# Four interleaved streams in place of three, with extra products in the differential attention's steps

## The reference

```
x += attn0(norm(x))   # causal, 8 heads of 16, with a bias of head directions ("geo")
x += ffn0(norm(x))    # 8 experts, top 1, hidden 512                          ("moe0")
x += attn1(norm(x))   # differential: per token, 32 x 32 scores over heads of 4,
                      # two softmaxes, one minus lambda times the other, rmsnorm ("diff")
x += relu mlp(norm)   # hidden 512 (part of the same layer)                    ("ff")
x += ffn1(norm(x))    # rows and weights quantised to a 6-bit grid in blocks of 32 ("mx")
x += attn2(norm(x))   # 16 heads of 8, q, k, v, o with low-rank additions      ("lora")
x += ffn2(norm(x))    # 14 experts, top 1, hidden 256                         ("moe2")
x += attn3(norm(x))   # causal, 16 heads, 128-wide q and k, values of 8        ("wide")
out = x + ffn3(norm(x))  # 8 experts, top 1 with a capacity over all tokens, hidden 128 ("moe3")
```

## Time and profile before

| | us |
|---|---|
| median of three runs | 3001.14 |
| profiled execution, its own time | 2994.16 |
| its span, first to last instruction | 2992.9 |
| PE / DVE / ACT / POOL busy | 1949.1 / 1711.6 / 1148.7 / 667.2 |
| granted TensorE clock, mean | 0.757 |
| one of the six three-stream rounds | 323.3 to 328.4 |

### The profile page before, as it was taken

One profiled execution on the slowest core, in us unless ns is written; L12 is line 12 of the kernel. 1 busy time (PEld: TensorE's weight loads), 2 busy tenths in 40 slices (PEclk: granted clock), 3 DMA queues, 4 the chain that ended last, 5 costly groups with the idle time before them and its releaser, 6 DMA issues. The chain is left out here.

```text
span 2992.9 us, 42119 instructions
## 1 busy us (share of the span) xinstructions
PE 1949.1 (65%) x12945; PEld 1395.1 (47%) x12945; DVE 1711.6 (57%) x4319; ACT 1148.7 (38%) x2756; POOL 667.2 (22%) x900
## 2 busy tenths in 40 slices
PE   4540655588756785598657876679559866666483
PEld 3330442456454564466444655456346635443352
DVE  2337545666584667665675668466766667552132
ACT  0320323255433463265333553355325543243251
POOL 1015002500243103500251014310350025201101
PEclk9875865688757895699668985699569876785795
DMA  6120040304141322305140324223230514011402
GB/s 177 37 78 0 13 122 6 111 6 102 52 120 40 64 73 77 100 7 125 33 138 13 73 70 115 57 42 96 69 108 1 126 34 133 15 23 44 128 1 60
DMA packets 265524, 201.28 MB, mean 67 GB/s; under 512 B 29668, under 2 KB 238692, under 8 KB 264708
## 3 DMA queue, kind: packets, MB, share of 16 engines
q1 hardware_dynamic: 259124, 185.59, 24.1%
q0 software_dynamic: 6144, 12.60, 1.5%
HBM read 151.58 MB, written 35.52 MB: 63 GB/s over the span
## 5 line engine op out<-in xcount | busy, mean ns | idle before, releaser
L1607 DVE TENSOR_REDUCE mid_room<-ps 128x2 f32<-128x512 f32 x256 | 165.2, 688 | 104.1 <-PE ps L944 101.2
L1200 ACT ACTIVATE late_room<-ps 128x384 f32<-128x384 f32 x256 | 125.9, 492 | 244.2 <-PE ps L875 242.3
L1212 ACT ACTIVATE late_room<-ps,late_neg_max 128x128 f32<-128x128 f32 (+1 forms) x512 | 187.3, 421 | 32.1 <-DVE late_neg_max L1582 27.6
L1047 PE MATMUL ps<-mid_pool 128*128 128x128 f32 x544 | 134.0, 390 | 97.4 <-DMA mid_pool<-moe_small 60.1
L1246 ACT ACTIVATE mid_room<-ps 128x512 f32<-128x512 f32 x256 | 140.2, 595 | 94.8 <-PE ps L955 94.8
L1763 DVE TENSOR_TENSOR early_pool<-ps,early_pool 128x1024 f32<-128x1024 f32 x128 | 150.8, 1220 | 37.2 <-ACT early_pool L1302 32.7
L1047 PEld LDWEIGHTS ps<-mid_pool 128*128 128x128 f32 x544 | 107.6, 275 | 122.1 <-DMA mid_pool<-moe_small 73.9
L865 PE MATMUL ps<-late_aT,heads_T 128*128 128x256 f32 x512 | 162.2, 400 | 0.0
L1284 ACT ACTIVATE mid_room<-ps,mid_pool 128x128 f32<-128x128 f32 x272 | 85.2, 364 | 188.8 <-PE ps L1047 188.1
L1770 DVE TENSOR_REDUCE early_pool<-early_pool 128x256 f32<-128x1024 f32 x128 | 149.8, 1212 | 1.3
L1581 DVE TENSOR_REDUCE late_neg_max<-ps 128x1 f32<-128x128 f32 x256 | 73.6, 287 | 125.8 <-PE ps L867 124.7
(11 more groups left out here) (374 smaller groups left out, 5088.0 us busy)
## 6 DMA issues: line engine op xcount, KB each, us to landing
mid_pool<-in_m_w_dram SPq DMA_DIRECT2D x272, 128.0 KB, 2.1
early_pool<-m_folded_w SPq DMA_DIRECT2D x88, 256.0 KB, 3.3
early_pool<-in_m_w_dram SPq DMA_DIRECT2D x88, 256.0 KB, 3.2
mid_pool<-mid_room SPq DMA_DIRECT2D x192, 64.0 KB
heads_T<-in_m_w_dram SPq DMA_DIRECT2D x176, 64.0 KB, 1.9
mid_pool<-moe_small SPq DMA_DIRECT2D x136, 65.0 KB, 1.9
mid_room<-moe_sorted_in SPq DMA_DIRECT2D x32, 256.0 KB, 3.1
moe_sorted_out<-mid_room SPq DMA_DIRECT2D x32, 256.0 KB, 2.5
```

Of the source, the lines that this page charges most:

```text
L1047: mm = pe.matmul(ps[:, B + b % h_banks, c * P:(c + 1) * P], table[:, c * P:(c + 1) * P], rows_T[s][:, b, :], start=True, stop=True)
L1200: act.activation(probs_T[s][:, k % (2 * QUAD), :], ps[:, s.last_bank, 0:3 * P], ACT.Copy)\
L1212: ins = act.activation(probs[s][:, n % RING, qt, 0:w], ps[:, bank, qt * P:qt * P + w], ACT.Exp, bias=neg_max[s][:, n % RING, qt:qt + 1])
L1607: dve.tensor_reduce(all_max[:, :, (h % 2 * 8 + h // 2) * GROUP_SEQS + seq], ps[:, B + n % S_BANKS, :].rearrange("p (q k) -> p q k", q=2), ...
```

## The change

- A fourth stream, SECOND, with PSUM bank 2 alone, takes diff from EARLY and ff and mx from MID. EARLY keeps geo and moe0 with banks 0 and 1; MID keeps lora and moe2; LATE is as before. Each order string is new, and there is one more round: EARLY; EARLY, SECOND; EARLY, SECOND, MID; five rounds of all four; SECOND, MID, LATE; MID, LATE; LATE.
- The ring of score banks is `s.banks - 1` for the causal attentions: one bank for geo, two for wide. Lora keeps two. `h_banks` of moe0 becomes one.
- Diff's q, k and v are copied from the one bank to a ring of three in SBUF by ACT, and the next product may start when that is done. DVE reads q, k and v there, and multiplies and sums one quarter at a time, the sum waiting for the product. ff too uses one bank where it had two.
- In the ten steps of each of diff's five passes PE does two products of 128 x 512 in bfloat16 in most steps, into SECOND's bank between its uses, which nobody reads: 2 in each of four steps of all five passes, and 2 in each of two more steps of the last four, 56 in a round.
- Geo's q and k are copied whole, and PE takes the 17 rows of a head from them; the strips and POOL's clearing are gone. Values are packed without padding.
- A block's table is one DMA from a table laid out whole in DRAM in the preparation, into a ring of three. The tables of moe2 and moe3 are laid out by DMAs on ACT's queue beside the first round, and SP waits for them after it.
- In the causal attentions ACT copies the summed values after the exponentials of the step and not before.
- At a round's end there are three copies of x and none of z.

```diff
-TABLES = 4
-TABLE_DMAS = 3
+TABLES = 3
...
+    def score_banks(self, at):
+        return self.banks if at is LORA else self.banks - 1
...
-EARLY = Stream("early", 0, 3, ["geo_in", "geo_out", "moe0_router", "diff_in", "diff_out"],
-               ["v", "o", "conn"])
-MID = Stream("mid", 3, 2, ["diff_ff", "mx_in", "lora_in", "lora_out", "moe2_in"], ["ff", "mx", "v", "o"])
+EARLY = Stream("early", 0, 2, ["geo_in", "geo_out", "moe0_router"], ["v", "o"])
+SECOND = Stream("second", 2, 1, ["diff_in", "diff_out", "diff_ff", "mx_in"], ["conn", "ff", "mx"])
+MID = Stream("mid", 3, 2, ["lora_in", "lora_out", "moe2_in"], ["v", "o"])
 LATE = Stream("late", 5, 3, ["wide_in", "wide_out", "moe3_router"], ["v", "o"])
...
+    "ESML": (
+        "MLMMESELMLSEMMELSLEEMLSELEMSLLESLEMLLEMLMESLLMESMLMELMLELMELMLEMLMLEEMLEMLLMEMLMEMMMMMESMESMMSSME"
...
-                    sp.dma_start(tables[s][:, i, 0:m.w2_at], layer1[m][:, bass.ds(expert, 1), :]).then_inc(here, 16)
-                    sp.dma_start(tables[s][:, i, m.w2_at:m.b2_at],
-                                 layer2[m][:, bass.ds(expert * m.chunks, m.chunks), :]).then_inc(here, 16)
-                    sp.dma_start(tables[s][:, i, m.b2_at:m.width],
-                                 small[m][bass.ds(expert * P, P), :]).then_inc(here, 16)
+                    sp.dma_start(tables[s][:, i, :].unsqueeze(1), whole[m][:, bass.ds(expert, 1), :]).then_inc(here, 16)
...
+                    ring = s.score_banks(at)
+                    if k >= ring:
+                        before_kind, before_n = slots[k - ring]
...
+                    def keep_busy(n):
+
+                        for _ in range(n):
+                            pe.matmul(ps[:, B, :], ones_bf[:, :],
+                                      tri[:, :].unsqueeze(1).broadcast_to([P, BANK // P, P]), start=True, stop=True)
 
                     def qkv(t):
-                        if t >= 2:
-                            pe.wait_ge(qkv_used, t - 1)
-                        pe.matmul(ps[:, B + t % 2, 0:3 * DIM], aT[s][:, t * P:(t + 1) * P], diff_w[:, :],
+                        if t >= 1:
+                            pe.wait_ge(qkv_kept, t)
+                        pe.matmul(ps[:, B, 0:3 * DIM], aT[s][:, t * P:(t + 1) * P], diff_w[:, :],
                                   start=True, stop=True).then_inc(qkv_ready, 1)
...
+                        for _ in range(2):
+                            if t >= 1:
+                                keep_busy(2)
+                            yield
+                        if t + 1 < TILES:
+                            qkv(t + 1)
+                        yield from steps(4)
+                        pe.wait_ge(qkv_kept, min(t + 2, TILES))
+                        for _ in range(len(DIFF_PARTS) - 6):
+                            keep_busy(2)
+                            yield
...
                         settle()
-                        for i in quarters:
-                            tick(dve.tensor_tensor(
-                                prod[:, i % 2, :, :].rearrange("p (i j) d -> p i j d", i=n),
-                                q[:, i * n:(i + 1) * n, :].unsqueeze(2).broadcast_to(shape),
-                                k.broadcast_to(shape), ALU.mult))
...
+                        link(dve.tensor_tensor(
+                            prod.rearrange("p (i j d) -> p i j d", i=n, j=DIFF_Q),
+                            q[:, i * n:(i + 1) * n, :].unsqueeze(2).broadcast_to(shape),
+                            k.unsqueeze(1).broadcast_to(shape), ALU.mult))
+                        tick(dve.tensor_reduce(dscores[:, i * 256:(i + 1) * 256],
+                                               prod.rearrange("p (n d) -> p n d", d=DIFF_D), AX.X, ALU.add))
...
-        with nc.Fori(0, GROUPS - 2) as g:
+        with nc.Fori(0, GROUPS - 3) as g:
             with nc.Block(no_gpsimd_drain=True) as block:
-                group_block(block, [EARLY, MID, LATE], x_v[:, bass.ds(g * TILES + 2 * TILES, TILES), :],
+                group_block(block, list(STREAMS), x_v[:, bass.ds(g * TILES + 3 * TILES, TILES), :],
```

More of the change, by code:

```diff
@@ L285, in sequence_model @@
             rstd[s] = own("rstd", [P, 2, TILES])
-            v_pad[s] = own("v_pad", [P, TILES, heads, STRIP])
+        for s, at, m in ((EARLY, GEO, MOE0), (MID, LORA, MOE2), (LATE, WIDE, MOE3)):
+            own = lambda name, shape, dt=F32: sb(f"{s.name}_{name}", shape, dt)
+            v_pad[s] = own("v_pad", [P, TILES, at.heads * (at.v_depth + 1) + STRIP])
             inv_sum[s] = own("inv_sum", [P, 16, 1])
@@ L634, in _ @@
             def _(act):
-                act.wait_ge(lam_ready, 1)
+                act.wait_ge(prepared, LAM)
                 act.activation(lam_exp[:, :], lam_sum[:, :], ACT.Exp).then_inc(lam_exped, 1)
+                act.wait_ge(weights_here, LOADED)
+                for dst, src in later_copies:
+                    with nc.allow_non_contiguous_dma(reason="columns of tables, once"):
+                        act.dma_start(dst, src).then_inc(later_tables, 16)
             @block.vector
@@ L759, in early, with second @@
                     yield from experts(EARLY, MOE0)
-                    yield from steps(len(WEIGHTS[EARLY]) - len(causal_weights(EARLY, GEO))
-                                     - len(experts_weights(MOE0)))
+                def second():
+                    yield from steps(len(WEIGHTS[SECOND]))
                 def mid():
-                    yield from steps(len(FF_STEPS))
                     yield from steps(4)
@@ L804, in _ @@
                     sp.wait_ge(x_here, 16)
-                take_steps(streams, [early() if s is EARLY else mid() if s is MID else late() for s in streams])
+                programs = {EARLY: early, SECOND: second, MID: mid, LATE: late}
+                take_steps(streams, [programs[s]() for s in streams])
             @block.tensor
@@ L1105, in early @@
                     yield
-                def mid():
-                    s, B = MID, MID.bank
                     yield from steps(2)
```

359 lines of the change are left out of this document (180 added, 179 removed).

## The result

The changed kernel takes 2949.47 us (median of 4 runs, 2940.5 to 2953.44), the kernel before beside it 2998.9 (2990.37 to 3003.38). The ratio is 0.9865, 95% interval 0.9815 to 0.9914: faster by 1.35%, where 6.4% was forecast. It lies outside the forecast's own range (2720 to 2910) and nearest to the 2974 of the rival "little gained". The page of the changed kernel answers to the earlier trace rows.

A forecast was written before the change was run, and what follows sets the result against it. Too few independent chains for two in-order engines were taken as the bound. Rounds outside the full ones, 1346 us, plus five full rounds, 1455, made 2801; with span and run offsets 2809 us, 6.4% less, range 2720 to 2910.

The forecast's parts named there:

- little gained: Rival for the full rounds: rate only 1.42, 324 us a round, 2974 us in all; chance 0.15.
- The more independent chains stand in the string, the less often: Bound of the kernel before: in-order engines wait at their heads; rate 0.8, 1.1, 1.36 with one, two, three streams.
- With four I take 1.56: Five full rounds: PE plus DVE work over length 1.56, within 1.46 and 1.75, giving 291 us a round.
- up to 21 us: Geo's single score bank: up to 21 us more in EARLY alone, or in a full round if uncovered.
- under 8 us in a full round if hidden: Check on PE's waits for ACT's exponentials at the score products: under 8 us if hidden, over 20 for the slower rival.
- Slower: the single banks hold PE: Rival for the full rounds: rate stays 1.36, 345 us a round, 3079 us in all; chance 0.15.
- more than 40 us from 1346: Sign of a wrong prediction: rounds of filling summing to more than 40 us away from 1346.
- EARLY alone was 151: First round: 55 + 71 us for geo and moe0, plus up to 21 and 4 for single banks, 151.
- MID, LATE was 228: Round of MID and LATE without ff and mx: 144.8 + 83.6 = 228 us.
- Nothing in the sum: One DMA per table: 3 us gain a round (0 to 8), a ring of three giving some back (0 to 5).
- The work of DVE: Full rounds: DVE's quarters stay at 1.22 us each for product and sum; waiting adds up to 0.1 us x 16.
- The extra products: The 56 unread products in a full round: 18 us of PE as cost, 10 as gain by a better clock.

The follow-up runs named there:

- e6: Changed kernel with the ESML string of the full rounds replaced by one spreading each stream's steps evenly; 3233.33 us, 1.0784.
- e7: Kernel before, three streams, with its EML string replaced by an evenly spread one; 3448.78 us, 1.1512.
- e8: Kernel before with one score bank for geo, one for moe0's first layer, and ACT's copy of out_T behind the exponentials; 3157.45 us, 1.051.
- e9: Changed kernel with ACT's exponentials ahead of the copy of probs_T in geo; 2950.13 us, 0.9856.
- e4: Changed kernel with three banks for EARLY (two for scores) in the three rounds where LATE does not run; 2917.89 us, 0.9749.
- e15: e12 plus e14's ring of four and a third bank for MID in rounds where EARLY or LATE does not run; 2836.32 us, 0.946.
- e12: Changed kernel with the edits of e3, e4 and e5 together; 2875.96 us, 0.9611.
- e14: Changed kernel with a ring of four tables for moe2 and moe3, three kept for moe0; 2949.97 us, 0.9845.
- e13: Kernel before, ring of four tables kept, with each table fetched by one DMA from whole tables in DRAM; 2980.54 us, 0.9944.
- e3: Changed kernel with ACT's copy turning diff's v so that DVE reads it in order; 2934.53 us, 0.9816.
- e1: Changed kernel without the 448 products that nobody reads; 2941.46 us, 0.9839.
- e2: Kernel before with the same 56 unread products a round added in EARLY's last bank during diff; 2996.37 us, 1.0016.
- e5: Changed kernel with four steps of EARLY and SECOND moved ahead of six of MID's in ESML; 2946.23 us, 0.9824.
- e11: Changed kernel with each table fetched by three DMAs of column ranges, ring of three kept; 3054.32 us, 1.0205.

## Why the prediction was right in sign and wrong in size

**The mechanism.** "The more independent chains stand in the string, the less often" an engine stands still: PE plus DVE over length rose from 1.36 to 1.46, and with even orders the same step takes 34 us from a round (e6, e7). That much fits. That the fourth chain alone does it is not shown, since no run has four streams and nothing else changed. The sum over rounds is right as a method: of the seven parts outside, three came within 6 us.

**The step that failed** is "With four I take 1.56". The full rounds measured 1.46, 307.7 us instead of 291, which is 83 of the 149 us. The work in the sum was right (450 us for 454), so the error is the rate. It continued a series of 0.8, 1.1, 1.36 with "each added less than the one before", but the steps it names (0.26, then 0.26 to 0.3) do not get smaller, and the series says nothing of a fourth step that also takes banks away. Its own lower bound, 1.46, is what came.

Why the rate stopped there is open. The prediction had worked out a price of single banks, "up to 21 us" for geo and 13 for moe0, and put it "inside the 1.56", in no term of its own. In e8 single banks cost some 20 us in each round of three streams, and it shows as PE's wait for ACT at geo's score products (13.4 us). But e8 runs the order of the kernel before, which has two banks, and it moves ACT's copy of the summed values too, which no run tries alone. In the changed kernel's full round PE never waits for ACT at geo's score products; its waits for geo's exponentials come at the value products, 3.9 us in all, and moe0's first layer has no wait for ACT:

```profile
PE ps L897 <- ACT early_room L1233: 3.9, 3, 1.3
```

The check "under 8 us in a full round if hidden" therefore says hidden, and e9, which shortens the chain, wins nothing there. 307.7 less 20 would be 288, next to the 291 forecast, but that is arithmetic with a number of another order and not a finding. It may be that the new string bends around the single bank at a price that no row of waits shows; nothing here tests it. What the rows do show of PE's idle time in that round are waits for other things: 11.4 us for MID's normalised rows, 8.4 for SECOND's rows behind the quantised layer, 7.9 for tables, 7.6 for the rows of maxima.

**The rivals.** "Little gained" came nearest in time, 2974 us, with 1.42 and 324 us for a full round. It had too low a rate in the full rounds and too little time outside them, and the two partly cancel. "Slower: the single banks hold PE" had 345 us a round; its sign, over 20 us of waits for ACT at the score products, did not come.

**The rounds of filling.** By the prediction's own sign (more than 40 us from 1346) it is wrong here: 1412. EARLY alone was 151 and took 183.8. The chain of 2.6 to 2.7 us a unit is right to the tenth at the full clock. The terms carried over from the earlier trace rows are not: geo's stretch ran at 0.96 there and at 0.61 here, and took 97 us for 55, where 21 more were taken:

```profile
82.30:179.30 97.00, 62.00 (x248) 35.04 (x248) 17.71 (x62) 21.93 (x56) 1.28 (x2) 0.61 0.01 3
```

The prediction took PE's work as unchanged, and in e4, with two banks and PE never idle, the clock is at 0.50 all the same. Against the 126 us of the earlier trace rows the round is 58 longer, and e4 takes 31 of them back. Moe0 took some 85 us for 71, where 4 more were taken; PE waits 12.0 us for its tables in this round, 6.4 in the kernel before. MID, LATE was 228 and took 243.4: the forecast added up the lengths of lora's and moe2's stretches, in which PE is busy 138 us, while all of LATE's work falls into the new round, which has 164. EARLY, SECOND, MID was 260 and took 277.7, with 364 us of work at 1.31. That MID's two banks bind in both is what e15 says beside e12 (256.0 for 269.9 and 224.2 for 243.4), in which only the ring differs besides, and e14's ring alone left them at 276.9 and 239.5.

**Tables by one DMA.** "Nothing in the sum", with 0 to 8 us a round as bounds: measured 15.5 us in a full round, 17 in MID, LATE, 105 in the launch. The bound was made from PE's wait for tables with three streams (6.4 us), and there the saving is 2 us a round (e13), as taken. It was not asked what the transfers cost when a fourth stream's work stands in the same queues. PE's wait for tables did not fall to the 3 us expected; it is 7.9. Put together, the result comes apart as follows: four streams with three DMAs cost 59 us (3054.32 against 2995.64 beside it), and the one DMA gives 105 back. Without this term, which the sum had at nothing, the change would have been slower than the kernel before.

**The work of DVE** was taken as 1.22 us for each quarter. The product with v takes 2.07 from SBUF, and DVE is busy 217 us in a full round instead of 211. e3 takes that back without a gain that is clear of the noise.

**The extra products** were taken as 18 us of cost and 10 of gain. As PE time the net is right: PE is busy 7 us a full round more than in e1 (233.5 for 226.3), and the line of the 56 products in a full round reads:

```profile
L1098 PE MATMUL ps<-tri,ones_bf 128*128 128x512 bf16 x56 | 19.6, 458 | 0.0
```

On the clock the changed kernel has 0.85 in a full round and e1 0.83: it was high without them, probably because diff no longer stands alone. By the Trainium skill, "TensorE: Matmul & The Clock Gate", section "What's actually happening", activity is what releases the throttle. The trace of e2 agrees (0.77 to 0.84); the 32 us of e4 with PE always busy and the clock at 0.50 do not, and there the measurement decides. Neither says that the released clock buys time, and here it does not.

**Order.** The prediction left it out. The existing strings are worth 76 and 58 us a round against one even order each, in the launch far more than the whole change. Whether 1.56 could be reached by a better string is open: e5, one hand-made repair, won nothing that is clear of the noise.

## What to carry to other kernels

When a change adds a chain by taking buffers from the others, price the buffers as their own term and give it a sign; do not let it vanish in a rate read where the buffers were still there. Taking a buffer away alone prices it, but for the order that the kernel has then (e8), and the price need not hold under another. In rounds of filling and draining, buffers of the streams that are not running are free; using them brought 32 us for one stream (e4) and 40 for another (e15 over e12, a longer ring with it), more together than the whole change had. An edit that comes along as nothing in the sum, like the one DMA for a table, wants its own run: here it carried the sign of the result. A raised TensorE clock is no gain in itself: look at the round, not at the clock.

## What the runs showed of the hardware

A DVE product of 1024 floats read from SBUF in steps of eight floats takes 2.07 us, with the same floats in order 1.31, and from PSUM in steps of eight before 1.22. By the Trainium skill, "SBUF — State Buffer", section "Door 1: The DMA port swizzle", an access that crosses to a new line of 16 bytes pays a penalty, so four-byte elements can be strided freely only within four; steps of 32 bytes are beyond that, and the 0.76 us between the rows agrees.

Splitting a DMA in three without moving a byte more cost 15.5 us a round with four streams (e11) and 2 with three (e13), in kernels that differ in their rings and orders too.

A PE that is never idle does not by itself have the full clock: in e4 it stood at 0.50 over 32 us of products without a gap, many of them of 17 rows, while in the kernel before the same stage with products of 128 rows had 1.00 and PE busy 14.8 of 18 us.
